# SAGE rounds of a graph network on transposed features, with the neighbour sum as one-hot products in PSUM

## The chip, the cores and the metric

The kernel runs on one core of a Trainium2 chip. The metric is the device time of one execution in microseconds; the median of three runs of the kernel before is 15,159.25 us (15,142.46 to 15,169.26). TensorE is PE here, VectorE DVE, ScalarE ACT, GpSimd POOL, SyncE SP.

## The reference, cut to what matters

There are 100,000 nodes with 128 features in f32 and 50,000 edges, sorted by destination. The destinations are drawn as 100,000 u^2, so that low nodes have many edges. Four blocks follow each other, each as `x = layernorm(x + block(x))`:

```python
# block 0: two SAGE layers, L2-normalised          (rounds 0 and 1)
agg = segment_sum(x[src], dst); cnt = segment_sum(ones, dst)
out = (agg / max(cnt, 1)) @ W_l + b_l + x @ W_r
h   = relu(out / max(norm(out), 1e-12))
# block 1: four SAGE layers without the norm        (rounds 2 to 5)
h = relu(agg * inv_deg @ W_l + h @ W_r + bias)
# block 2: attention with a softmax over each node's edges (round 6), block 3: transformer conv (round 7)
# then batch norm and the last layer norm           (output pass)
```

Rounds 0 to 5 are the six SAGE rounds; the layer norms of blocks 0 and 1 belong to rounds 1 and 5.

## The kernel before, in words

**Preparation.** The edges are loaded as a table of 98 blocks of 512. DVE, PE and POOL sort them by source in two passes (for round 6), and build index tables for gathers (`idx`), marks of equal neighbours (`keep`) and `inv`, one over the rank of an edge in its destination. `unit_end` says up to which unit of nodes the edges of a pair of blocks reach.

**A SAGE round** works in rows of nodes in DRAM and goes over 49 pairs of edge blocks (`schedule`, L377). For each pair POOL gathers source rows by indirect DMA, 128 rows an instruction (`gathers`, L592), PE transposes them into `edge_bank` (L731), DVE runs a scan along the edges (L1310: the running sum starts anew at each destination), PE multiplies by W_l (L737), ACT scales the rows by `inv` (L905), and POOL scatters those that close a destination into `agg` in DRAM (L603). SP waits until the scatters of the pair before have landed (L514) and only then loads.

**The dense part** goes in units of 1,024 nodes (98 of them, each two groups of 512 nodes, `s` = 0, 1) as soon as the edges below them are done. SP loads h (L520) and agg (L526) by groups, PE transposes h (L821), ACT copies it to SBUF (L968), PE adds bias (L827) and h W_r (L830), DVE adds the aggregate (L1428), and a tail follows by kind of round: norm, norm and layer norm, ReLU (ACT, L990), or ReLU and layer norm. ACT issues the stores (L961).

**Order.** Each engine runs its program in order. In an engine's program the pair comes first and then the units that it frees, so that a late unit holds up the next pair and the other way round. The tiles `h_in`, `agg_in`, `h_t`, `total`, `h_out` are doubled by `s` and are reused unit by unit. Rounds 6 and 7 (GAT and TR) have the same frame with a softmax in place of the scan. They keep their code in the change.

## Time and profile before

| | us |
|---|---|
| median of 3 runs | 15,159.25 |
| lowest, highest | 15,142.46, 15,169.26 |
| span of the profiled execution | 18,775.6 |
| PE busy in it | 9,112.1 (49%) |
| PE weight loads | 6,508.0 (35%) |
| DVE busy | 7,851.5 (42%) |
| POOL busy | 7,388.1 (39%) |
| ACT busy | 5,083.3 (27%) |
| DMA packets | 1,168,749, 2,071 MB, 110 GB/s |

The profiled execution has no other time than its span on record; what lies around the span isn't shown. The span is 3,616 us above the median of the other runs. Busy is the time in which the engine works on instructions; an engine that is idle may wait for another (then the profile names the releaser where it can) or for a DMA. "remote" and "issue" are waits for which it shows no releaser. The granted TensorE clock is a share of 2.4 GHz: 0.5 is 1.2 GHz; its mean over the run is 0.651.

### The profile page before, as it was taken

The numbers are of one execution on the slowest core, as the hardware profiler recorded it, in microseconds if no ns is written. First come the engines' busy times: TensorE is split into PE (matmuls) and PEld (weight loads), VectorE is DVE, ScalarE is ACT, GpSimd is POOL, SyncE is SP. The second block draws the span as 40 slices with busy tenths as digits, with TensorE's granted clock in tenths as the row PEclk, the third lists the DMA queues.
The fourth block names the chain that finished last, engine by engine and source line by source line (L and its number), as shares of the span: only waits on it lengthen the run. The fifth ranks groups of instructions, "written<-read, shape, count | busy, mean of one in ns | idle before, by whom it ended". The sixth has DMA issues, their size and how long they took to land. (4 is left out here: it accounts for less than half of the span.)

```text
span 18775.6 us, 221914 instructions
## 1 busy us (share of the span) xinstructions
PE 9112.1 (49%) x39191; PEld 6508.0 (35%) x39290; DVE 7851.5 (42%) x24729; ACT 5083.3 (27%) x12365; POOL 7388.1 (39%) x7460
## 2 busy tenths in 40 slices
...
GB/s 227 1 3 1 67 121 147 116 102 120 130 130 75 121 151 122 103 144 164 73 138 162 93 137 157 176 110 98 98 97 97 97 53 51 68 79 88 102 163 233
DMA packets 1168749, 2071.11 MB, mean 110 GB/s; under 512 B 283745, under 2 KB 292466, under 8 KB 1155794
## 3 DMA queue, kind: packets, MB, share of 16 engines
...
q14 instruction: 39, 0.32, 0.0%
...
HBM read 1358.91 MB, written 772.63 MB: 114 GB/s over the span
## 5 line engine op out<-in xcount | busy, mean ns | idle before, releaser
L603 POOL DMA_INDIRECT agg<-y_rows,s_idx x3136 | 3130.6, 998 | 1994.0 <-issue 1222.1
L827 PE MATMUL o_bank<-b_parts,ones_parts 3*128 3x512 bf16 (+1 forms) x1568 | 826.8, 527 | 4417.7 <-ACT h_t L968 2347.8
L830 PE MATMUL o_bank<-w_r,h_t 128*128 128x128 f32 x12544 | 2803.8, 393 | 0.0
L830 PEld LDWEIGHTS o_bank<-w_r,h_t 128*128 128x128 f32 x12544 | 2394.3, 285 | 577.3 <-issue 576.7
L1428 DVE TENSOR_TENSOR total<-o_bank,agg_in 128x512 f32<-128x512 f32 (+1 forms) x1568 | 1038.2, 688 | 3305.4 <-DMA agg_in<-agg 2001.8
L594 POOL DMA_INDIRECT gath<-node_a,g_idx x1176 | 1133.2, 964 | 2528.2 <-DVE g_idx L1292 1221.5
L968 ACT ACTIVATE h_t<-ht_bank 128x512 f32<-128x512 f32 (+1 forms) x1568 | 884.3, 593 | 3821.8 <-remote 2628.7
L827 PEld LDWEIGHTS o_bank<-b_parts,ones_parts 3*128 3x128 bf16 (+1 forms) x1568 | 150.5, 96 | 4800.6 <-ACT h_t L968 3073.7
L594 POOL DMA_INDIRECT gath<-node_b,g_idx x784 | 776.4, 990 | 2153.0 <-DVE g_idx L1292 1358.7
L594 POOL DMA_INDIRECT gath<-node_x,g_idx x784 | 782.7, 998 | 2052.7 <-DVE g_idx L1292 1161.4
L905 ACT ACTIVATE y_rows<-edge_bank,inv 128x128 f32<-128x128 f32 x2352 | 667.0, 369 | 2775.5 <-remote 1090.3
L1310 DVE TENSOR_TENSOR_SCAN run<-keep,run,edge_bank 128x512 f32<-128x512 f32 (+1 forms) x588 | 752.5, 1280 | 1307.6 <-PE edge_bank L731 604.1
L737 PE MATMUL edge_bank<-w_l,run 128*128 128x128 f32 x4704 | 895.2, 358 | 744.3 <-DVE run L1310 739.7
L821 PE MATMUL ht_bank<-ident,h_in 128*128 128x128 f32 x6272 | 1138.8, 339 | 230.1 <-issue 114.0
L582 POOL DMA_INDIRECT rec_dram<-rec_rows,place_idx x784 | 754.8, 963 | 1154.9 <-DVE rec_rows L1249 927.7
L1037 ACT ACTIVATE h_out<-t,small 128x128 f32<-128x128 f32 x2744 | 1096.9, 480 | 87.9 <-DVE small L1417 52.9
L821 PEld LDWEIGHTS ht_bank<-ident,h_in 128*128 128x128 f32 x6272 | 982.7, 182 | 366.0 <-issue 261.1
L737 PEld LDWEIGHTS edge_bank<-w_l,run 128*128 128x128 f32 x4704 | 800.7, 260 | 853.0 <-DVE run L1310 843.6
L731 PE MATMUL edge_bank<-ident,gath 128*128 128x128 f32 x2352 | 476.9, 361 | 813.8 <-DMA gath<-node_a,g_idx 403.0
L747 PE MATMUL edge_bank<-ident,run 128*128 128x128 f32 x784 | 218.6, 434 | 1318.7 <-DVE run L1347 1303.2
L1433 DVE TENSOR_REDUCE small<-zeros 128x4 f32<-128x512 f32 x392 | 262.1, 684 | 1157.1 <-ACT zeros L980 591.8
L731 PEld LDWEIGHTS edge_bank<-ident,gath 128*128 128x128 f32 x2352 | 398.2, 194 | 855.5 <-DMA gath<-node_a,g_idx 422.8
...
## 6 DMA issues: line engine op xcount, KB each, us to landing
...
node_x<-h_out ACTq DMA_DIRECT2D x390, 256.0 KB
h_in<-node_x SPq DMA_DIRECT2D x390, 256.0 KB
node_b<-h_out ACTq DMA_DIRECT2D x390, 256.0 KB
h_in<-node_b SPq DMA_DIRECT2D x390, 256.0 KB
...
```

The source lines that it names most:

```text
L582: pool.indirect_dma_start(rec_dram[n], bass.IndirectOffsetOnAxis(place_idx[q][:, k:k + 1], 0), rec_rows[q][:, k, :], None).then_inc(rec_ou ...
L594: pool.indirect_dma_start(gath[q][:, k, :], None, h_of, bass.IndirectOffsetOnAxis(g_idx[q][:, k:k + 1], 0)).then_inc(gathered[q], 16)
L603: pool.indirect_dma_start(agg[order(r)], bass.IndirectOffsetOnAxis(s_idx[q][:, k:k + 1], 0), y_rows[q][:, k, :], None, bounds_check=N - 1, ...
L731: last = pe.transpose(pe_bank[q][:, k * P:(k + 1) * P], gath[q][:, k, :], ident[:])
L737: last = pe.matmul(pe_bank[2 + q][:, k * P:(k + 1) * P], run[q][:, k * P:(k + 1) * P], w_l[r][:], start=True, stop=True, skip_group_check= ...
L821: last = pe.transpose(ht_bank[s][:, j * P:j * P + p], h_in[s][0:p, j, :], ident[0:p, 0:p])
L827: pe.matmul(o_bank[s][0:p, :], ones_parts[:, 0:p], b_parts[:, r, :].unsqueeze(1).to_broadcast([3, RPP, P]), start=True, stop=False, skip_g ...
L830: last = pe.matmul(o_bank[s][0:p, j * P:(j + 1) * P], h_t[s][:, j, 0:p], w_r[r][:], start=False, stop=j == RPP - 1, skip_group_check=True)
L968: act.activation(h_t[s][:, :, 0:p], ht_bank[s][:].rearrange("p (j n) -> p j n", j=RPP)[:, :, 0:p], ACT.Copy).then_inc(ht_ready[s], 1)
L1037: last = act.activation(h_out[s][0:p, j, :], of[s][0:p, j, :], ACT.Identity, scale=small2[s][0:p, 2 + 2 * turn, j:j + 1], bias=small2[s][0 ...
L1310: dve.tensor_tensor_scan(run[q][:], keep_of(i, q), pe_bank[q][:], run[1 - q][:, BLOCK - 1:BLOCK], ALU.mult, ALU.add).then_inc(run_ready[q], 1)
L1428: dve.tensor_tensor(flat(total[s], p), o_bank[s][0:p, :], flat(agg_in[s], p), ALU.add).then_inc(sum_ready[s], 1)
```

## The change

Rounds 0 to 5 get a program of their own; rounds 6 and 7 and the output pass stay, apart from names of semaphores.

- **Transposed features.** h is kept as columns in DRAM: for each of 196 groups a [128 features x 512 nodes] tile (`h_even`, `h_odd`, `n_cols`, `x_cols`), with node 4 p + j of the group at column 128 j + p. Loads and stores of it need no transpose. Round 0 has x in rows: PE transposes it and SP also stores it as columns, for the residual of round 1.
- **W_l at the writing side.** Beside the columns each round writes rows `y = h W_l(next round)`, 256 KB a group (`y_even`, `y_odd`), which the next round gathers. So the sum over neighbours needs no product any more. Round 0 gathers x itself and applies W_l after the sum. Round 5 writes plain rows (`node_b`) for round 6.
- **One-hot sums.** The edges are seen as 391 blocks of 128. For each group PE multiplies every block that touches it (`held`: gathered rows times 1 / degree, 128 x 128) by a one-hot matrix (`pick`: 128 edges x 512 nodes), both built by DVE, and adds into one PSUM bank; W_r h goes into the same bank (in round 0 into another). A block that spans a group's border is visited by both, 586 visits a round. How many blocks a group has is read from `visit_tab` by every engine at run time; the staged pairs lie in A, B, C0, C1, D0, D1, and DVE can be two visits ahead of PE.
- **POOL** only gathers: 392 indirect DMAs a round, eight at a time, into a ring of 32 blocks. There are no scatters and no `agg` in these rounds.
- **Statistics by PE.** Squared norms and variances are products with a column of ones, four a group; the reciprocals are spread over the features by products with a broadcast; the mean is taken off by a product with `centre`. ACT takes the square roots and squares, DVE the reciprocals and the products of whole tiles.
- **SP** issues all transfers of these rounds, stores too. The steps of a group are staggered over engines by fixed lags (`S_LAG` to `H_LAG`).
- `inv` becomes one over the degree for every edge of a destination (`end_f`), and the tables `dst_tab` and `visit_tab` are added.

```diff
+    EB = EPAD // P
+    LASTB = (E - 1) // P
+    VISITS = LASTB + GROUPS
+    RING = 32
...
+        def visits(eng, i, m, visit):
+            g = group_of(i, m)
+            place = visit_tab[0:1, g:g + 1] if isinstance(g, int) else visit_tab[0:1, bass.ds(g, 1)]
+            packed = eng.value_load(place, min_val=0, max_val=LASTB * 512 + 511)
+            lo, count = packed >> 9, packed & 511
...
+            visit(g, block_of(lo), f"C{m % 2}", True)
+            pairs = count >> 1
+            with eng.If(pairs > 0):
+                with eng.Fori(0, pairs) as n:
+                    visit(g, block_of(lo + (2 * n + 1)), "A", False)
+                    visit(g, block_of(lo + (2 * n + 2)), "B", False)
+            with eng.If((count & 1) > 0):
+                visit(g, block_of(lo + count), f"D{m % 2}", False)
...
+        S_LAG = {R_X: 2, R_NLN: 1}
+        C_LAG = {R_NLN: 2, R_RLN: 1}
+        T_LAG = {R_NLN: 3, R_RLN: 2}
+        O_LAG = {R_X: 1}
+        Y_LAG = {r: {R_X: 3, R_NLN: 4, R_RLN: 3}.get(r, 1) for r in sage_rounds}
+        H_LAG = {r: {R_X: 3, R_NLN: 4, R_RLN: 3}.get(r, 1) for r in sage_rounds}
...
+                            sp.wait_ge(o_mm[0], o_mm.at(r, g - 3))
+                            sp.sem_inc(sp_turn, 1)
+                            sp.dma_start(hin[q], cols_of(h_source[r], g)).then_inc(group_in[q], 16)
...
+                        cols_ready = relu_done if r in relu_sage else h_done
+                        sp.wait_ge(cols_ready[0], cols_ready.at(r, group_of(i, m) + 1))
+                        sp.sem_inc(sp_turn, 1)
+                        sp.dma_start(cols_of(h_target[r], group_of(i, m)), h_cols[m % 2]).then_inc(h_cols_out[m % 2], 16)
...
+                        sp.wait_ge(y_done[0], y_done.at(r, group_of(i, m) + 1))
+                        sp.sem_inc(sp_turn, 1)
+                        sp.dma_start(rows_of(y_table[r + 1], group_of(i, m)), as_cols(y_out[m % 2])).then_inc(y_rows_out[m % 2], 16)
...
+            def eight_blocks(r, d, turn_of_ring):
+                done = r * EIGHTS + d
+                pool.wait_ge(released, (done + 1) * 8)
+                pool.sem_inc(pool_turn, 1)
+                near = near_idx[turn_of_ring]
+                pool.tensor_copy(near[:].rearrange("p (b k) -> p b k", k=CPB),
+                                 idx[0][:, bass.ds(2 * d, 2), 0:CPB]).then_inc(copied, 1)
+                pool.wait_ge(copied, done + 1)
+                pool.sem_inc(pool_turn, 1)
+                for half in range(2):
+                    for k in range(half * 4, half * 4 + 4):
+                        pool.indirect_dma_start(ring[:, turn_of_ring * 8 + k, :], None, y_table[r],
+                                                bass.IndirectOffsetOnAxis(near[:, k:k + 1], 0)).then_inc(blocks_in[half], 16)
+                    if half == 1:
+                        pool.wait_ge(blocks_in[0], (done + 1) * 64)
+                        pool.sem_inc(block_ready, 4)
...
+                def visit_into(bank):
+                    def visit(g, b, name, first):
+                        pe.wait_ge(staged, r * VISITS + b + g + 1)
+                        pe.matmul(bank[:], held[name], pick[name], start=first, stop=False, skip_group_check=True).then_inc(used, 1)
...
+                        pe.matmul(bank[:], w_r[r][:], hin[m % 4], start=False, stop=True, skip_group_check=True).then_inc(o_mm[0], 1)
...
+                def column_sums(bank, of, weight):
+                    for j in range(RPP):
+                        last = pe.matmul(bank[:, j:j + 1], of[:, j * P:(j + 1) * P], weight[:], start=True, stop=True,
+                                         skip_group_check=True)
...
+                def spread(bank, values):
+                    for j in range(RPP):
+                        last = pe.matmul(bank[:, j * P:(j + 1) * P], values[:, j:j + 1].to_broadcast([P, P]), ident[:],
+                                         start=True, stop=True, skip_group_check=True)
...
+                def step(i, k):
+                    if r in two_norm and running(i, k - S_LAG[r]):
+                        square_sums(i, k - S_LAG[r])
+                    if r in two_ln and running(i, k - C_LAG[r]):
+                        centred(i, k - C_LAG[r])
+                    if running(i, k):
+                        aggregated(i, k)
+                    if r == R_X and running(i, k + 1):
+                        x_columns(i, k + 1)
+                    if r in two_norm and running(i, k - S_LAG[r]):
+                        unit_spread(i, k - S_LAG[r])
+                    if r == R_X and running(i, k - 1):
+                        both_products(i, k - 1)
+                    if r in two_ln and running(i, k - C_LAG[r]):
+                        variances(i, k - C_LAG[r])
+                    if r in two_ln and running(i, k - T_LAG[r]):
+                        scale_spread(i, k - T_LAG[r])
+                    if running(i, k - Y_LAG[r]):
+                        next_rows(i, k - Y_LAG[r])
...
+                def visit(g, b, name, first):
+                    dve.wait_ge(block_ready, r * EB + b + 1)
+                    dve.wait_ge(used, r * VISITS + b + g + 1)
+                    slot = (b + r * EB) & (RING - 1)
+                    scaled = dve.tensor_scalar(held[name], ring[:, bass.ds(slot, 1), :].rearrange("p o f -> p (o f)"),
+                                               column(inv_tab, b), None, ALU.mult)
+                    if not first:
+                        scaled.then_inc(released, 1)
+                    dve.tensor_scalar(pick[name], iota_node[:], column(dst_tab, b), column(group_off, g),
+                                      ALU.subtract, ALU.is_equal).then_inc(staged, 1)
...
+                def step(i, k):
+                    if running(i, k):
+                        visits(dve, i, k, visit)
+                    if r in two_norm and running(i, k - S_LAG[r]):
+                        unit_scales(i, k - S_LAG[r])
+                    if r in two_ln and running(i, k - T_LAG[r]):
+                        scales(i, k - T_LAG[r])
+                    if r in two_norm and running(i, k - S_LAG[r]):
+                        unit_rows(i, k - S_LAG[r])
+                    s_lag = S_LAG[r] if r == R_NLN else 0
+                    if r in two_ln and running(i, k - s_lag):
+                        residual_sum(i, k - s_lag)
+                    if r in two_ln and running(i, k - T_LAG[r]):
+                        normalised(i, k - T_LAG[r])
...
-                    for step, q in ((gathers, 0), (gathers, 1), (scatters, 0), (scatters, 1)) if kind != SAGE else (
-                            (gathers, 0), (scatters, 0), (gathers, 1), (scatters, 1)):
...
-                def sage_pair(i, r=r):
```

On ACT a group costs: round 0 a square root, the copy of the sum, the copy of the transposed x, square, ReLU, copy of the next rows; round 1 square root, square and copy of the centred tile, square, ReLU, square root, next rows; a ReLU round ReLU and next rows.

## Rows read from the trace of the kernel before

**Rows 1.** Stages: window, us, busy by engine (instructions), clock, DMA share, GB/s
```profile
270.00:1958.30 1688.30, 968.39 (x3900) 365.18 (x3998) 932.02 (x3571) 0.00 (x0) 754.79 (x784) 0.72 0.03 6
1958.30:3578.70 1620.40, 789.73 (x3724) 634.25 (x3724) 628.82 (x1864) 369.73 (x982) 769.26 (x784) 0.65 0.39 121
3578.70:5763.70 2185.00, 900.66 (x3724) 731.64 (x3724) 1014.21 (x4021) 802.90 (x2149) 769.68 (x784) 0.60 0.37 114
5763.70:10438.30 4674.60, 2293.36 (x11172) 1837.11 (x11172) 852.58 (x1477) 992.00 (x2359) 2306.79 (x2352) 0.67 0.41 127
10438.30:12249.30 1811.00, 846.03 (x3724) 679.47 (x3724) 744.88 (x2846) 566.60 (x1569) 772.68 (x784) 0.63 0.44 141
12249.30:15125.80 2876.50, 1140.81 (x4508) 844.69 (x4508) 2081.50 (x6666) 1295.79 (x3039) 788.39 (x784) 0.58 0.32 98
15125.80:18775.60 3649.80, 2170.78 (x8428) 1413.37 (x8428) 1569.51 (x4222) 1053.57 (x2257) 1224.02 (x1176) 0.67 0.34 104
1958.30:12249.30 10291.00, 4829.77 (x22344) 3882.47 (x22344) 3240.47 (x10205) 2731.24 (x7058) 4618.41 (x4704) 0.64 0.40 126
```
**Rows 2.** Waits in rounds 2 to 4: us in total, times, longest us
```profile
DVE total L1428 <- DMA agg_in<-agg: 1477.1, 274, 21.7
ACT h_t L968 <- remote: 1401.5, 222, 14.4
POOL gath L594 <- PE edge_bank L731: 1275.5, 100, 26.3
```
**Rows 3.** One transfer in POOL's timeline, round 3: start, us, operation, idle before
```profile
7954.85 1.02 POOL L603 DMA_INDIRECT agg<-y_rows,s_idx  x1 [0.30 <-issue]
```
**Rows 4.** Timeline of SP's transfers in round 2
```profile
6497.68 0.92 SPq L526 DMA_DIRECT2D agg_in<-agg  x2
6506.85 4.93 SPq L520 DMA_DIRECT2D h_in<-node_x  x2
6516.80 4.94 SPq L526 DMA_DIRECT2D agg_in<-agg  x2
```
**Rows 5.** Timeline of PE in round 6
```profile
13505.65 1.71 PE L749 MATMUL edge_bank<-head_pick,den 128*128 128x4 f32 x8
...
13512.40 1.88 PE L767 MATMUL edge_bank<-gsrc_t,w_t 128*128 128x512 f32 x4
13514.11 1.04 PE L821 MATMUL ht_bank<-ident,h_in 128*128 128x128 f32 x8
...
13516.05 1.16 PE L830 MATMUL o_bank<-w_r,h_t 128*128 128x128 f32 x8
```
**Rows 6.** Single lines: duration ns min/median/max, first and last start, forms
```profile
L1443 DVE TENSOR_SCALAR h_out<-total,small x784: 267/282/548, 2141.4 to 3578.5; 128x128 f32<-128x128 f32 x195, 40x128 f32<-40x128 f32 x1
...
L1177 DVE TENSOR_SCALAR keep<-keep x1: 426/426/426, 273.4 to 273.4; 98x512 f32<-98x512 f32 x1
...
L1224 DVE TENSOR_SCALAR keep<-keep x784: 283/343/551, 461.3 to 1901.2; 128x512 bf16<-128x512 f16 x98, 128x264 bf16<-128x264 f16 x98
...
L1428 DVE TENSOR_TENSOR total<-o_bank,agg_in x1568: 673/691/694, 2131.1 to 18107.7; 128x512 f32<-128x512 f32 x196
...
L990 ACT ACTIVATE h_out<-total x784: 612/629/633, 5944.5 to 18108.4; 128x512 f32<-128x512 f32 x196
```
**Rows 7.** DVE's operations of the sorter's line L1218 in 20 us of the trace
```profile
300.00:320.00 20.00, 16.29 (x47) 1.00 0.00 0
```
**Rows 8.** Line L385 (the read of a table at run time), sequencer of DVE
```profile
L385 DVEq TENSOR_LOAD <-unit_end x384: 299/309/1033, 1974.3 to 17980.2; - x192
```
**Rows 9.** Stretches as in group 1: sorting twice, then the output pass
```profile
320.00:440.00 120.00, 116.37 (x488) 54.41 (x557) 98.15 (x279) 0.00 (x0) 0.00 (x0) 1.00 0.00 0
1173.00:1280.00 107.00, 96.86 (x722) 58.07 (x720) 84.45 (x386) 0.00 (x0) 10.64 (x12) 0.96 0.00 0
18530.00:18630.00 100.00, 54.50 (x240) 48.89 (x240) 70.23 (x360) 74.73 (x180) 0.00 (x0) 0.53 0.74 235
```
**Rows 10.** Line L594, the gathers: duration ns min/median/max
```profile
L594 POOL DMA_INDIRECT gath<-node_a,g_idx x1176: 942/953/1128, 3581.4 to 12108.4; - x196
```

675 lines of the change are left out of this document (506 added, 169 removed).

## The prediction

> **What bounds the kernel now.** I read the stages first, then who waits in them, then single operations. The stages [rows 1] cut the profiled span of 18,776 us at the start of each round: 270 us of loading and zeroing, 1,688 us of sorting, six SAGE rounds, 2,877 us for the attention round, 3,650 us for the transformer round with the output pass. The SAGE rounds take 10,291 us, and they are all that the change rebuilds; the reader is to see that in them no engine is busy for more than half of the time (PE 4,830, POOL 4,618, DVE 3,240, ACT 2,731 us). So they are bound by waits. In the three plain ReLU rounds [rows 2] DVE waits for the aggregate to come back from DRAM (1,477 us of 4,675), ACT for a transposed tile whose load is late (1,402 us, releaser not seen), POOL for the transposes behind the dense units on PE's in-order queue (1,276 us). That is a chain through DRAM: gather, scan, scatter, then load of what was scattered.
>
> A floor under it is POOL: 16 gathers and scatters for each of 49 pairs at 1.28 us each (0.98 busy on average, 4,618 us for 4,704 of them [rows 1], and 0.30 of issue [rows 3]) are 784 x 1.28 = 1,004 us in every round, against 1,558 us for a ReLU round.
>
> One thing must be said of the profile. Its span is 24% over the median of the timed runs (15,159 us); no row shows what lies around the span. Where the excess sits is partly seen [rows 4]: two loads that SP normally issues in 0.92 us take 4.93 and 4.94 us, while POOL is in the middle of its gathers. I come back to this, as it decides the sign.
>
> **The change, priced.** Removed from the rounds: the scans, the 392 scatters of a round, the reload of the aggregate, the transposes of each dense unit, and all unit statistics on DVE. Added: 390 + 196 = 586 visits a round (a block of 128 edges against a group of 512 nodes), and dense work for 196 groups in transposed form.
>
> PE, at its full clock. The nearest rows [rows 5]: four 512-column f32 instructions go by in 13514.11 - 13512.40 = 1.71 us, and an f32 product is two of them, so 0.86 us; four 128-column products (8 instructions) last 1.04 to 1.16 us with the tail of the last, 0.9 from start to start. Column sums (8 weight loads, hardly any columns) are 1.71 us at the low clock, so about 0.85 at the full one. By group, with 2.99 visits on average:
> - ReLU round: 3.99 x 0.86 (visits, W_r) + 0.9 (next rows) = 4.33 us; x196 = 849 us, three times.
> - Round 0: 4.99 x 0.86 (visits, W_r, W_l) + 3 x 0.9 (transposes, spread, next rows) + 0.85 (sums) = 7.84; 1,537 us.
> - Round 1: 4.99 x 0.86 (visits, W_r, centring) + 2 x 0.85 + 3 x 0.9 = 8.69; 1,703 us.
> - Round 5: 4.99 x 0.86 + 0.85 + 2 x 0.9 = 6.94; 1,360 us.
> Together 3 x 849 + 1,537 + 1,703 + 1,360 = 7,147 us. Nothing hides this: it is one engine in order. The bounds are the full clock (7,147) and the low clock throughout (twice that).
>
> DVE, visits. One multiplication of 128x128 f32 with a column as scalar is 282 ns; the comparison over 512 columns is 426 ns with constants, some 45 more with two columns as operands [rows 6], so 0.28 + 0.47 = 0.75 us. Register work comes on top: the sorter's loop issues 47 such operations in 20 us [rows 7], 0.43 us each where one lasts 0.35, so 0.08 for each. With two waits I take 1.05 us a visit, between 0.75 (all registers hidden) and 1.3. Per group the visit table is read: 0.31 us for the load, then unpacking, two branches and a loop [rows 8], 1.3 us taken, between 0.5 and 2.1. So 2.99 x 1.05 + 1.3 = 4.4 us in a ReLU round, as much as PE has. With only two buffers for a staged visit (`used` starts at 2) the two engines can't fully even out; I add 0.4 us a group there. In round 0 DVE has 0.17 + 0.17 + 0.69 more, in round 1 0.52 + 3 x 0.69, in round 5 0.17 + 2 x 0.69: under PE's sums, but DVE stands still for PE's spread products, and what is queued behind on DVE is the next group's first visit, for which PE then waits. I add 0.2, 0.5 and 0.5 us. Sum: 0.4 x 588 + 0.2 x 196 + 0.5 x 392 = 470 us.
>
> ACT has at most six 512-column passes of 0.6 us a group [rows 6], 3.6 us, and is hidden under PE everywhere; without PE's cover it would be the limit of no round. SP now issues the stores too: three transfers (four in round 0) at 0.6 us each with their registers, 1.9 to 2.5 us a group, hidden. If SP goes slow as in [rows 4], the three groups loaded ahead cover some 13 us; the stores have two buffers, so ACT's rectified tile and, behind it, PE's next product would wait. DMA: 0.79 MB a group in 4.4 us is 180 GB/s; the output pass moves 235 GB/s at a share of 0.74 [rows 9], so hidden.
>
> POOL: 392 gathers x 1.28 = 502 us and 49 copies with waits, about 575 us a round, under every round. But destinations are crowded at low nodes (their density falls as one over the root of the position), so the first 15 groups need some 107 blocks, and there POOL's 1.4 us a block exceeds the visit's 1.05: 40 us a round. Each round also drains its stores and fills the ring, 35 us. Together 6 x 75 = 450 us.
>
> After: 7,147 + 470 + 450 = 8,067 us for the SAGE rounds against 10,291. The table work before them is one-off and small (some 20 operations under 1 us, inside 1,688 us). In the profile's own time that is 18,776 - 10,291 + 8,067 = 16,552 us.
>
> **A rule that speaks against it.** The longest case of the one-column multiplication is 548 ns against 282 typical, and of the sorter's comparison 551 against 343 [rows 6], and the sorter's fell beside POOL's transfers: DVE and POOL do disturb each other here, by up to 0.27 us. The visits put two such operations beside POOL's gathers all the time. The Trainium skill (SBUF — State Buffer, "SBUF: two separate sides") says that a VectorE operation in a two-port mode takes a port pair exclusively, so that GpSimd can't write descriptors until it ends; its own example is a transfer of 620 ns that takes 3,100. By that factor a gather would take five times as long. By the rows, the 1,176 gathers from node_a last 0.94 to 1.13 us [rows 10], so POOL's side hardly shows it; I charge nothing for it in the sum and keep it as rival 4.
>
> **From the profile to the timed runs.** The rest of the program shrinks by 15,159 / 18,776 = 0.807 if the excess is spread evenly: 8,485 becomes 6,850 us. PE's instruction rate cannot shrink, the other 920 us of the new rounds can: 7,147 + 743 = 7,890. Sum 14,740 us, 2.8% faster. That is the forecast.
>
> **Rivals.**
> 1. *The excess sits in the old SAGE rounds* (slower). Then they take far less than 8,309 us when timed, and the new PE-bound rounds replace something cheap. The point is 7,890: if more than 2,401 of the 3,617 us of excess is theirs, the change loses. For it: the slow SP issues [rows 4] are in these rounds beside POOL's bursts, and late loads are what the rounds wait for [rows 2]. Against: POOL alone needs 1,004 us in each, 6,024 in all, rounds 1 and 5 have long DVE chains above it, and 1,688 us of sorting also run beside POOL. With 3,000 us of it there: 15,159 + (7,890 - 7,291) = 15,760 us.
> 2. *PE doesn't hold its full clock* (slower). The granted clock is 1.00 in a stretch in which PE is busy for 97%, 0.96 at 91%, 0.53 at 54% [rows 9]; the SAGE rounds now have 0.64. If the two-buffer handshake leaves PE at 80% busy and the clock at 0.8 on average, PE's 7,147 become 8,930: 16,500 us. It decides from a mean clock under 0.94 (7,147 / (7,147 + 419)). The forecast has PE busy for 89%, so the rows speak for a clock near 1. The Trainium skill (TensorE: Matmul & The Clock Gate, "HAM oscillation — how this bites in real kernels") tells of loops whose regular waits throw the array back to half rate; the trace agrees where waits are long.
> 3. *The visits are cheaper, and the old profile stretches all alike* (faster): everything goes by 0.807, (8,485 + 8,067) x 0.807 = 13,360 us. For it: register and semaphore work is what a profile would stretch; against: matmul spacing is not.
> 4. *POOL starves the visits*: each gather waits for a whole comparison of DVE, 1.28 + 0.47 = 1.75 us. 686 us a round is still hidden later on, but the crowded groups get 107 x 0.47 us more, 300 us in all: 15,040 us. For it: the stretched operations of [rows 6]; against: [rows 10]. By the factor of five in the Trainium skill's example (SBUF — State Buffer) POOL would bind every round at 392 x 6.4 us, and the time would be near 22,000 us; no row is near that.
>
> **How the numbers follow.** Forecast 0.50, rival 1 0.21, rival 2 0.10, rival 3 0.12, rival 4 0.07. A measurement of this kernel tells 0.2%, some 30 us, from no change. The forecast's own range is 14,100 to 15,400: DVE's visit at 0.75 or 1.3 us takes 235 us off or puts 280 on in the ReLU rounds, and the waits on spread products and round ends (about 680 us of the sum) can be none or twice that, not all on one side together. A tenth of it lies above 15,190. Faster: 0.42 of the forecast, rivals 3 and 4, together 0.61. Same: 0.03 of the forecast and 0.02 of rivals 1 and 2. Slower: 0.05 and 0.29, together 0.34. The range takes in most of rivals 1 and 3: 13,400 to 16,100.
>
> **What would show it.** Right: ReLU rounds near 1,000 us and rounds 0, 1, 5 near 1,650, 1,880, 1,540; PE busy over 85% in them with a clock over 0.95; a visit's cadence of 1.0 to 1.1 us. Wrong: PE waiting for the comparison with DVE over 90% busy (my visit is too cheap); a clock near 0.7 (rival 2); DVE waiting for `ring` past the first 15 groups, or gathers well over 1.3 us (rival 4); ACT waiting for h_cols or y_out stores (SP). If the profiled rounds come out at 8,000 to 8,500 us and the timed run is still slower, rival 1 is right.

## The result: 3.1% slower where it was first compared, 2.3% faster on another chip

| | kernel before, us | kernel after, us | after / before |
|---|---|---|---|
| first comparison (4 runs each) | 15,150.85 (15,129.81 to 15,169.26) | 15,622.35 (15,607.41 to 15,638.28) | 1.0309 [1.0297, 1.0321] |
| a later one, on another chip | 18,445.97 (7 runs) | 18,022.38 (4 runs) | 0.977 [0.9749, 0.9791] |

The forecast of 14,740 us was wrong, and in sign: the change costs 3.1% where it was to be measured. The kernel before takes 15,150 to 15,170 us on some chips and 18,450 to 18,790 us on others, within 0.4% in each set of runs, and each ratio below compares two kernels on one chip. I call them the quick and the slow chips; whether it is the chip itself or what runs beside it there, the runs don't tell. The profile that the prediction rests on has the span of a slow one (18,776 us), the times beside it are those of a quick one. The unaltered changed kernel ran on one chip of each kind.

The stages of the changed kernel on a quick chip (window, us, busy time of PE, PEld, DVE, ACT, POOL with instructions, PE's clock, DMA share, GB/s), cut at the starts of the rounds: the sorting, rounds 0, 1, 2, 5, then all six SAGE rounds.

```profile
270.00:1635.00 1365.00, 907.02 (x4008) 349.34 (x4008) 939.94 (x3594) 0.94 (x2) 752.84 (x785) 0.82 0.03 3
1635.70:3345.50 1709.80, 1643.29 (x7836) 1021.45 (x7836) 637.40 (x1760) 610.45 (x1176) 391.62 (x442) 1.00 0.41 135
3345.50:5216.30 1870.80, 1818.30 (x9796) 1204.82 (x9796) 921.51 (x2348) 663.19 (x1372) 390.59 (x441) 1.00 0.40 124
5216.30:6169.20 952.90, 902.00 (x3132) 454.50 (x3132) 448.21 (x1172) 251.73 (x392) 393.71 (x441) 0.99 0.59 189
...
8071.70:9764.80 1693.10, 1515.75 (x6660) 849.69 (x6660) 734.23 (x1760) 516.01 (x980) 392.69 (x440) 1.00 0.35 106
...
1635.70:9764.80 8129.10, 7684.98 (x33688) 4441.23 (x33688) 3634.96 (x9384) 2544.82 (x4704) 2355.51 (x2645) 1.00 0.46 145
```

Against [rows 1] the picture is another one: TensorE is busy for 95% of the six rounds at a granted clock of 1.00 (before: 47% at 0.64, and 57% at 0.73 in the quick profile below), and POOL's 784 transfers a round have become 441 operations (392 gathers, 49 copies). The rounds take 8,129 us, 0.8% from the 8,067 of the sum. Yet the kernel is slower, since on this chip the old rounds were not the 10,291 us of [rows 1]. Below is a second profile of the kernel before, from a quick chip (span 15,168.7 us; the same columns; rounds 0, 1, 2 and 5, then all six):

```profile
1634.90:2811.30 1176.40, 723.95 (x3724) 584.33 (x3724) 627.39 (x1865) 367.56 (x982) 768.52 (x784) 0.75 0.52 167
2811.30:4597.80 1786.50, 836.96 (x3724) 682.91 (x3724) 1016.43 (x4021) 801.63 (x2149) 767.95 (x784) 0.65 0.45 139
4597.80:5749.70 1151.90, 708.63 (x3724) 570.57 (x3724) 289.04 (x494) 337.89 (x791) 767.40 (x784) 0.74 0.53 171
...
8019.60:9332.40 1312.80, 751.87 (x3724) 605.38 (x3724) 748.34 (x2846) 571.92 (x1570) 781.97 (x784) 0.72 0.59 195
...
1634.90:9332.40 7697.50, 4400.31 (x22344) 3552.99 (x22344) 3260.49 (x10205) 2748.63 (x7058) 4620.62 (x4704) 0.73 0.52 168
```

Round by round, from these two tables (after less before, quick chips): round 0 +533 us (1,710 against 1,176), round 1 +84, rounds 2 to 4 -199, -185 and -182, round 5 +380. The six together +432, and the rest of the program 7,504 against 7,471. That is the 464 us between the spans (15,632.7 and 15,168.7). What was won in the ReLU rounds (566 us) is less than what rounds 0 and 5 lose (913 us).

Where PE's time goes in a round that loses can be read in its groups in round 0 of the changed kernel (line, engine, operation, tile, count | busy us, mean ns | idle before them and what ended it):

```profile
L979 PE MATMUL edge_bank<-keep 128*128 128x512 f32 x1172 | 598.2, 626 | 57.1 <-DVE keep L1750 39.5 <-issue 12.8
L990 PE MATMUL ht_bank<-ident,node_small 128*128 128x128 f32 x1568 | 207.4, 275 | 1.4 <-DVE node_small L1759 1.4
L1067 PE MATMUL edge_bank<-w_l,keep 128*128 128x128 f32 x1568 | 206.7, 275 | 0.8 <-ACT keep L1314 0.8
L984 PE MATMUL edge_bank<-one_col,keep 128*128 128x1 f32 x1568 | 206.1, 253 | 1.6 <-ACT keep L1286 1.6
L1036 PE MATMUL o_bank<-t,w_l 128*128 128x512 f32 x392 | 200.2, 592 | 0.0
```

The visits are only 598 of the 1,710 us. A norm in transposed form costs PE 413 us of busy time a round that it did not have before: 206 for the sums of squares (L984, one output column from each weight load of 128) and 207 to spread one value a node over its 128 features (L990). Before, DVE and ACT did this, and PE was busy for 62% of round 0. That this work is why round 0 loses is a sum of busy times, not a test; the last set of experiments speaks against it for the sums of squares.

### The profile page after: what moved, and what is told of

It reads as the page before. It is cut to its first block, busy times and chain, and to the rows that moved or that the text cites. A ratio compares the mean times of both kernels' runs of the same rounds, so it can differ in the third digit from the quotient of the medians.

```text
span 15632.7 us, 266007 instructions
## 1 busy us (share of the span) xinstructions
PE 11691.0 (75%) x50643; PEld 6945.8 (44%) x50644; DVE 8242.4 (53%) x23933; ACT 4902.6 (31%) x10013; POOL 5131.3 (33%) x5404
## 4 chain that ended last, share of the span: by engine, by line
PE 49%; DVE 19%; issue 11%; DMA 5%; DVEq 5%; POOL 5%; ACT 4%; SPq 1%; ACTq 1%; another core or an unknown queue 0%; POOLq 0%
PE o_bank L979 13%; PE o_bank L1019 5%; PE edge_bank L1067 5%; PE ht_bank L990 5%; PE edge_bank L984 3%; DVE keep L1750 3%; POOL rec_dram L782 3%; PE edge_bank L979 3%; DVE st L1934 2%; ACT t L1444 2%; PE edge_bank L934 2%; DVE seg_max L1855 2%; DVE full_max L1858 2%; DVE run L1882 2%; ACT h_out L1466 2%
## 5 line engine op out<-in xcount | busy, mean ns | idle before, releaser
L979 PE MATMUL o_bank<-keep 128*128 128x512 f32 x5860 | 3054.1, 624 | 372.2 <-DVE keep L1750 329.0
L1746 DVE TENSOR_SCALAR keep<-keep,inv 128x128 f32 x3516 | 1056.2, 300 | 2597.1 <-PE o_bank L979 1236.9
L1750 DVE TENSOR_SCALAR keep<-iota_node,dst_tab,group_off 128x512 f32<-128x512 f32 x3516 | 1947.8, 554 | 0.5 <-issue 0.4
L979 PEld LDWEIGHTS o_bank<-keep 128*128 128x128 f32 x5860 | 924.9, 190 | 2053.1 <-DVE keep L1750 1851.9
L799 POOL DMA_INDIRECT keep<-y_even,near_idx x1176 | 1142.2, 971 | 449.6 <-issue 316.8
L1067 PEld LDWEIGHTS edge_bank<-w_l,keep 128*128 128x128 f32 x7840 | 1013.8, 192 | 374.5 <-issue 364.7
L1067 PE MATMUL edge_bank<-w_l,keep 128*128 128x128 f32 x7840 | 1033.8, 275 | 1.6 <-ACT keep L1314 1.6
L843 POOL DMA_INDIRECT agg<-y_rows,s_idx x784 | 777.0, 991 | 707.0 <-DVE s_idx L1843 476.9
L799 POOL DMA_INDIRECT keep<-y_odd,near_idx x784 | 763.8, 974 | 303.4 <-issue 209.4
L990 PE MATMUL ht_bank<-ident,node_small 128*128 128x128 f32 x6272 | 860.0, 280 | 1.4 <-DVE node_small L1759 1.4
L990 PEld LDWEIGHTS ht_bank<-ident,node_small 128*128 128x128 f32 x6272 | 777.8, 190 | 95.7 <-issue 93.3
```

What stands on the lines that cost most here:

```text
L799: pool.indirect_dma_start(ring[:, turn_of_ring * 8 + k, :], None, y_table[r], bass.IndirectOffsetOnAxis(near[:, k:k + 1], 0)).then_inc(blo ...
L843: pool.indirect_dma_start(agg[order(r)], bass.IndirectOffsetOnAxis(s_idx[q][:, k:k + 1], 0), y_rows[q][:, k, :], None, bounds_check=N - 1, ...
L979: pe.matmul(bank[:], held[name], pick[name], start=first, stop=False, skip_group_check=True).then_inc(used, 1)
L990: last = pe.matmul(bank[:, j * P:(j + 1) * P], values[:, j:j + 1].to_broadcast([P, P]), ident[:], start=True, stop=True, skip_group_check= ...
L1067: last = pe.matmul(bank[:, j * P:(j + 1) * P], h_cols[m % 2][:, j * P:(j + 1) * P], weight[:], start=True, stop=True, skip_group_check=True)
L1746: scaled = dve.tensor_scalar(held[name], ring[:, bass.ds(slot, 1), :].rearrange("p o f -> p (o f)"), column(inv_tab, b), None, ALU.mult)
```

## The experiments

**First set, on a quick chip: where did the old kernel's time lie?** Rival 1 of the prediction says that the excess of the first profile sits in the old SAGE rounds. All four are the kernel before, or parts of it.

Unaltered, profiled again. 

> The kernel before, unchanged, profiled a second time. Its first profile has a span of 18,776 us where its timed runs take 15,151 us; the profile of the changed kernel has 15,633 us where it takes 15,622 us. Theory A (the excess of 3,617 us is an accident of one profiled execution): the span is now near 15,160 us, SP's pairs of transfers take 0.92 us everywhere, and the ReLU rounds are far under 1,558 us. Theory B (it belongs to this kernel under a profiler): the span is again near 18,800 us, with the same slow transfers beside POOL's bursts. Timed: 15,151 us in either case.

Measured: 15,166.93 us, ratio 1.0006 [0.9995, 1.0016]; its span is 15,168.7 us. So a profile does not stretch the kernel, and what theory A foretold holds. (The first profile is no accident of one execution, though: the later sets time this kernel at 18,446 to 18,794 us on other chips.) The register work that SP does before a load (L388) shows where the two profiles differ, first in the first profile, then here (count: shortest, median, longest ns):

```profile
L388 SPq FUSED_REGOPS  x724: 3/41/1395, 2124.9 to 18020.0; - x181
L388 SPq COMPARE_BRANCH  x724: 4/45/1425, 2139.5 to 18027.7; - x181
```
```profile
L388 SPq FUSED_REGOPS  x724: 41/41/51, 1775.3 to 14415.3; - x181
L388 SPq COMPARE_BRANCH  x724: 34/45/50, 1778.0 to 14421.2; - x181
```

The medians agree, the tails don't. Of the register and branch instructions in the old SAGE rounds, 901 of SP's 9,972 and 491 of ACT's 10,379 took over 0.45 us in the first profile (some 0.7 each), and none in the second.

The SAGE rounds left out.
```diff
-        (SAGE, "norm", x_in, None, node_a, ...),        # and the other five SAGE rows of ROUNDS
-        (GAT, "gat", node_b, node_b, node_x, ...),
+        (GAT, "gat", x_in, x_in, node_x, ...),
```


> The kernel before without its six SAGE rounds: round 6 reads x, all else stays. Theory 1 (the excess of the profile lay in the old SAGE rounds, these were cheap when timed): what is left takes what the same stages take in the profile of the changed kernel, 270 + 1,365 + 2,811 + 3,057 = 7,503 us, and the old SAGE rounds took 15,151 - 7,503 = 7,648 us. Theory 2 (the excess was spread evenly, and the changed kernel made the stages after it slower): 0.807 x 8,485 = 6,850 us, and the old SAGE rounds took 8,300 us.

Measured: 7,466.72 us (7,461.32 to 7,468.13), ratio 0.4928 [0.4919, 0.4936]. The old SAGE rounds are worth 15,157 - 7,467 = 7,690 us, not 8,309, if nothing overlaps at their ends.

Rounds 3 and 4 left out, and rounds 0 and 1 left out.
```diff
-        (SAGE, "relu", node_a, None, node_b, ...),
-        (SAGE, "relu", node_b, None, node_a, ...),
...
-        (SAGE, "norm", x_in, None, node_a, ...),
-        (SAGE, "norm_ln", node_a, x_in, node_x, ...),
-        (SAGE, "relu", node_x, None, node_a, ...),
+        (SAGE, "relu", x_in, None, node_a, ...),
```


> The kernel before with two of its three ReLU rounds left out (rounds 3 and 4; round 5 reads what round 2 wrote). Theory 1: a ReLU round is near POOL's floor of 784 x 1.28 = 1,004 us, say 1,030, so 15,151 - 2,060 = 13,090 us. Theory 2: a ReLU round takes 0.807 x 1,558 = 1,257 us, so 12,640 us. In the changed kernel it takes 952 us.

> The kernel before without rounds 0 and 1 (round 2 and the residual of round 5 read x). Together they take 3,581 us in the changed kernel. Theory 1: the old SAGE rounds sum to 7,648 us, of which 3 x 1,030 for ReLU rounds and some 1,500 for round 5, which leaves 3,060 us for these two: 12,090 us, so that nearly all of the loss is here (round 0 at 1,060 against 1,710 us). Theory 2: 0.807 x 3,805 = 3,071 us, 12,080 us. The two theories agree here; the run sizes rounds 0 and 1, and with the two other cuts also round 5.

Measured: 12,901.55 us (ratio 0.8522 [0.8507, 0.8536]) and 12,199.53 us (0.8055 [0.8041, 0.8068]): 1,128 us for a ReLU round, 2,957 for rounds 0 and 1, as in the second profile (1,135 and 2,963). A ReLU round had shrunk from 1,558 us to 1,135, by 0.728, not by the 0.807 that I gave to everything.

**Second set: what bounds the new rounds?** These are the changed kernel with one thing altered. They ran on a slow chip, where the kernel before took 18,460.34 us (7 runs); the changed kernel's own time to set beside them, 18,022, comes from the third set, on another slow chip whose kernel before stood at 18,446, so a difference of some tens of us says nothing.

The comparison of a visit over 128 of 512 nodes.
```diff
-   dve.tensor_scalar(pick[name], iota_node[:], ...
+   dve.tensor_scalar(pick[name][:, 0:P], iota_node[:, 0:P], ...
```


> From the changed kernel. VectorE's comparison of a visit is made over 128 of the 512 nodes of the group (the other 384 columns of the one-hot block stay zero, so most of the edge sums are left out); all other instructions, TensorE's full-width products among them, stay. In the profile of the changed kernel the comparison takes 554 ns on average, 3,516 times (1,948 us). Theory P (TensorE's own sum sets the SAGE rounds: it is busy 95% of them): VectorE waits longer, the time stays within 100 us of 15,620, as the ReLU rounds stay at about 950 us; at most the 175 us that TensorE idles in round 5 shrink. Theory V (the visits' hand-shake through VectorE sets them): about 0.4 us off each of 3,516 visits, 14,200 to 14,500.

Measured: 17,905.62 us, ratio 0.9689 [0.9673, 0.9706], 117 us under the changed kernel. DVE's comparison fell from 549 to 348 ns, 709 us of its work in all, and the time by a sixth of that. Theory V is out as it stood, and theory P's limit of 100 us is just passed.

A visit's product over 256 of 512 columns.
```diff
-   pe.matmul(bank[:], held[name], pick[name], ...
+   pe.matmul(bank[:, 0:GROUP // 2], held[name], pick[name][:, 0:GROUP // 2], ...
```


> From the changed kernel. TensorE's product of a visit covers 256 of the 512 columns of its PSUM bank (half of the edge sums is left out); VectorE's work stays whole. The product's two instructions take 614 to 646 ns each in the profile, 7,032 of them. Theory P: each pair loses up to 256 columns twice at full clock; by the 128x512 products (592 ns an instruction) against the 128x128 ones (275 ns for four times fewer columns) some 0.4 us a visit, 3,516 visits: 1,100 to 1,500 us off, 14,100 to 14,500, a ReLU round near 750. Theory V: no more than 150 us off, since VectorE's part of a visit is whole.

Measured: 17,561.37 us, ratio 0.9502 [0.9486, 0.9518], 461 us less: more than V's 150, far from P's 1,100.

bf16 for the squares and the columns that sum them.
```diff
-   one_col, mean_col = sb("one_col", [P, 1]), sb("mean_col", [P, 1])
+   one_col, mean_col = sb("one_col", [P, 1], BF16), sb("mean_col", [P, 1], BF16)
-   squares = [in_ring([GROUP]) for k in range(2)]       # and squares2
+   squares = [in_ring([GROUP], BF16) for k in range(2)]
```


> From the changed kernel. The squares whose sums over the features TensorE takes (one sum in the norm, one in the layer norm) are written in bf16, and their ones and 1/128 columns are bf16: each sum is then four bf16 products with four weight loads, where the f32 one is eight of each. In the profile a sum of a group takes 1.05 us of TensorE (1,568 instructions, 206.1 us in 196 groups), mostly for weight loads, and there are four such sums in rounds 0, 1 and 5 (784 groups together, 823 us). Theory P, with the norms' small products as what the norm rounds lose: a sum falls to 0.3 to 0.5 us, so 400 to 600 us off: 15,000 to 15,200, round 1 alone by 200 to 300, the ReLU rounds unchanged. Theory W (the extra time of rounds 0 and 5 is waiting between engines, not TensorE's work): under 100 us off.

Measured: 17,682.99 us, ratio 0.9565 [0.9547, 0.9584], 339 us less. In round 0 the sums went from 209.6 us on PE to 49.3, as these two lines show (the changed kernel, then this one):

```profile
L984 PE MATMUL edge_bank<-one_col,keep 128*128 128x1 f32 x1568 | 209.6, 255 | 33.6 <-ACT keep L1286 32.8 <-issue 0.8
```
```profile
L985 PE MATMUL edge_bank<-one_col,keep 128*128 128x1 bf16 x784 | 49.3, 167 | 31.7 <-ACT keep L1287 30.1 <-issue 1.6
```

That is 0.8 us of PE's busy time a sum and some 640 us in all, of which the time gave back about half: beside the changed kernel of the third set 156 us in round 1 and 155 in round 5, but 17 in round 0 (1,911 for 1,928).

A visit as two bf16 products, the block split in high and low part.
```diff
-   scaled = dve.tensor_scalar(held[name], block, inv, None, ALU.mult)
+   dve.tensor_scalar(held[name][:, 0, :], block, inv, None, ALU.mult).then_inc(hot, 1)
+   dve.wait_ge(hot, ...)
+   scaled = dve.scalar_tensor_tensor(held[name][:, 1, :], block, inv, held[name][:, 0, :], ALU.mult, ALU.subtract)
-   dve.tensor_scalar(pick[name], iota_node[:], ...     # f32
+   dve.tensor_scalar(pick[name], iota_half[:], ...     # fp16 in, bf16 out
-   pe.matmul(bank[:], held[name], pick[name], ...
+   pe.matmul(bank[:], held[name][:, 0, :], pick[name], ...
+   pe.matmul(bank[:], held[name][:, 1, :], pick[name], ...
```


> From the changed kernel. The scaled block of a visit is split on VectorE into two bf16 blocks (high part, and the rest), the one-hot block is written as bf16 from an fp16 row of node numbers, and the visit is two bf16 products in place of an f32 one, in all six SAGE rounds. Theory P: two bf16 products of 512 columns take TensorE about half of the f32 one's 1.25 us; 0.4 to 0.6 us off 3,516 visits; where the gathers (784 a round at 0.97 us, 760 us) or VectorE (three instructions a visit and a wait for its own result) don't catch it, 1,200 to 1,600 us off, ReLU rounds 760 to 850 us; forecast 14,300. Theory V: VectorE has one instruction and one wait more in each visit, the time rises by 500 to 1,000 us, unless its bf16 comparison is faster than 554 ns.

Measured: 18,257.59 us, ratio 0.9875 [0.9857, 0.9894], 235 us more than the changed kernel, though PE's busy time fell by 1,085 us (12,531 to 11,445). That is far from theory P and short of theory V. The third instruction costs DVE 351 ns, the bf16 comparison still takes 410.

**Third set, on another slow chip: does the sign hang on the chip?** The changed kernel again, the bf16 sums with a later layer norm in round 5, the high and low products again, all three together.
```diff
-   C_LAG = {R_NLN: 2, R_RLN: 1}
-   T_LAG = {R_NLN: 3, R_RLN: 2}
+   C_LAG = {R_NLN: 2, R_RLN: 2}
+   T_LAG = {R_NLN: 3, R_RLN: 3}      # Y_LAG and H_LAG of R_RLN 4, s_lag 1
```


> The changed kernel, unaltered, beside the kernel before. The last four kernels ran where the kernel before took 18,460 us, against 15,160 in the runs before them, and in their profiles some 1,060 to 1,130 of 40,700 register, branch and wait instructions of VectorE's sequencer and some 840 to 870 of SyncE's took over 0.45 us (median 0.04 us), against none and 16 in the profile of the changed kernel at 15,633 us. Theory M (a property of the chip or of what runs beside it, which stretches both kernels by a different amount, so that the sign of the change hangs on it): where the kernel before takes about 18,460 us, this one takes 18,100 to 18,400, the ratio 0.98 to 1.00, since its rounds 2 to 4 were 1,190 us there in the comparison over 128 nodes and rounds 0 and 5 some 1,900; where the kernel before takes about 15,160 us, the ratio is 1.030 again. Theory N (the changed kernel is 3% slower everywhere): 19,000 us at a kernel before of 18,460.

> The changed kernel with the squares and their columns in bf16 (as in the run of the bf16 sums) and round 5's layer norm one group later at each step, as in round 1. Theory P (TensorE's sum bounds the rounds, and round 5 loses 180 us more to a chain inside one group): where the kernel before takes 15,160 us, the sums give 400 to 600 us and the lag 50 to 150: 14,900 to 15,150, that is level with the kernel before or just below it; rounds 0, 1 and 5 at about 1,560, 1,570 and 1,400 us. Where the kernel before takes 18,460, it stays within 150 us of the run with the sums alone, 17,680. Theory W (waits between engines): the sums give under 100 us and only the lag counts.

> The changed kernel with the visits as two bf16 products (high and low part of the block), as run before. Where the kernel before took 18,460 us its rounds 2 to 4 took 1,240 us each, TensorE 65% busy and VectorE 46%, with 315 us a round in which VectorE's next block waited for nothing but its own sequencer. Theory D (a visit costs VectorE some 1.4 us in all: 0.29, 0.35 and 0.41 us of work and the registers and waits between, and this takes TensorE's place as the bound): where the kernel before takes 15,160 us, rounds 2 to 4 come to 586 visits x 1.4 = 820 to 950 us, the whole to 15,000 to 15,500. Theory P (TensorE's sum alone): 1,200 to 1,600 us off, 14,000 to 14,400.

> The changed kernel with all three: bf16 sums, bf16 high and low visits, round 5's layer norm one group later. Where the kernel before takes 15,160 us: by theory D, VectorE's 1.4 us a visit sets a floor of about 820 us in every round, and the norm rounds, where TensorE has 1,100 to 1,250 us of work left, gain both: 14,200 to 14,700. By theory P 13,600 to 14,000. Where the kernel before takes 18,460: the two bf16 products are no gain there, 17,500 to 17,900.

Measured, with the kernel before at 18,445.97 us: 18,022.38 (0.977 [0.9749, 0.9791]), 17,695.31 (0.958 [0.9554, 0.9607]), 18,230.55 (0.9875 [0.9855, 0.9895]) and 17,959.24 us (0.9733 [0.9713, 0.9753]). Theory M holds and its ratio was still a little too high: here the change gains 2.3%. The lag gives nothing here (17,695 against 17,683; round 5 takes 1,790 us with it and 1,795 with the sums alone), the three together are worse than the sums alone (17,500 to 17,900 was expected). The stages of the changed kernel here, rounds 0, 1, 2 and 5 and all that follows them (columns as above):

```profile
1928.00:3856.00 1928.00, 1722.63 (x7832) 1061.62 (x7832) 635.46 (x1760) 610.23 (x1175) 389.97 (x442) 0.94 0.36 120
3856.00:5988.00 2132.00, 1912.72 (x9796) 1243.59 (x9796) 922.09 (x2348) 656.70 (x1372) 389.64 (x442) 0.94 0.35 108
5988.00:7169.00 1181.00, 980.05 (x3132) 482.48 (x3132) 447.69 (x1172) 249.65 (x392) 391.41 (x442) 0.92 0.47 152
...
9565.00:11515.00 1950.00, 1627.23 (x6660) 922.16 (x6660) 734.50 (x1760) 513.65 (x980) 387.11 (x436) 0.92 0.30 92
11515.00:18018.60 6503.60, 3335.53 (x12936) 2255.36 (x12936) 3647.94 (x10888) 2353.59 (x5296) 2017.83 (x1960) 0.63 0.33 103
```

The new SAGE rounds go from 8,129 to 9,587 us (18% more), the old ones from 7,697 to 10,291 (34%). DVE's queue shows what does it, at the line that scales a block (quick chip, then this one):

```profile
L1746 DVEq ALU_OP  x6446: 40/45/50, 1644.0 to 9747.9; - x196
L1746 DVE TENSOR_SCALAR keep<-keep,inv x3516: 285/286/535, 1644.2 to 9748.1; 128x128 f32 x196
```
```profile
L1746 DVEq ALU_OP  x6446: 1/45/1408, 1929.1 to 11496.7; - x196
L1746 DVE TENSOR_SCALAR keep<-keep,inv x3516: 268/286/536, 1929.4 to 11496.9; 128x128 f32 x196
```

DVE's work on data takes what it took in the median; its register arithmetic has a tail. In the SAGE rounds 789 of DVE's 33,631 register and branch instructions took over 0.45 us (553 us together) and 421 of SP's, where the quick chip has none. The two engines hand visits to each other over two staging places, so PE's next product waits too. The granted clock goes with it: 0.92 over these rounds for 1.00, and PE's busy time grows from 7,685 to 8,218 us for the same instructions, 533 of the 1,458 us that are added.

**Fourth set, on a third slow chip** (kernel before 18,475.79 us).

> The changed kernel with the bf16 sums and round 5's layer norm one group later, as before, where the kernel before took 18,446 us and this one 17,695, against 18,022 for the changed kernel. Where the kernel before takes 15,160 us: theory P (TensorE's sum bounds the SAGE rounds there, 95% busy in them): 784 sums of about 0.6 us less are 470 us, more than the 327 us measured above, and the lag 50 to 150 us: 14,950 to 15,150. Theory W (waits between engines): 15,400 to 15,600. Where it takes 18,450: 17,700 again.

> The changed kernel with two bf16 products a visit, as before, where it cost 208 us more than the changed kernel (18,231 against 18,022). Where the kernel before takes 15,160 us: theory D (VectorE's part of a visit takes over as the bound, 1.06 us of work in three instructions and 0.3 to 0.4 us of registers, branches and the wait for its own result): ReLU rounds 820 to 950 us, in all 15,000 to 15,600. Theory P (TensorE alone): 14,000 to 14,400. Where it takes 18,450: 18,230 again.

> The changed kernel with the product of a visit over 256 of its 512 columns (half of the edge sums left out), as before, where it took 17,561 us, 461 less than the changed kernel. Where the kernel before takes 15,160 us: theory P: TensorE's busy time falls by some 250 us in each of six rounds, and the time by 1,100 to 1,500 us less what VectorE's visits (0.85 us of work and 0.3 to 0.4 us of registers and branches, 586 a round, 700 us) and the gathers (784 x 0.97 = 760 us a round) hold up: ReLU rounds at 760 to 800 us, in all 14,400 to 14,800. Theory V: within 150 us of 15,620. Where it takes 18,450: 17,560 again.

Measured: 17,707.04 (0.9577 [0.9552, 0.9602]), 18,282.18 (0.9891 [0.9863, 0.9919]) and 17,593.27 us (0.952 [0.9499, 0.9542]). They repeat the earlier ones within 0.3% and tell nothing of a quick chip.

**Fifth set: take the gathers away.** In the SAGE rounds of the third set's changed kernel, 85% of DVE's 789 slow instructions start within 1 us, before or after, of the start of one of POOL's indirect transfers, where 28% of all its register instructions do. So the gathers go, and with them, if that is the cause, the difference between the chips. All visits after the first 32 blocks read those blocks again, and the waits for the landings are set to be met at once.
```diff
+   first_ring = r == 0 and isinstance(d, int) and d < 4
...
-   for k in range(half * 4, half * 4 + 4):
+   for k in range(half * 4, half * 4 + 4 if first_ring else half * 4):
        pool.indirect_dma_start(ring[:, turn_of_ring * 8 + k, :], None, y_table[r], ...
...
-   pool.wait_ge(blocks_in[0], (done + 1) * 64)
+   pool.wait_ge(blocks_in[0], (done + 1) * 64 if first_ring else 256)      # and so for blocks_in[1]
```


> The changed kernel with 3,104 of its 3,136 gathers of the SAGE rounds left out: only the ring's first 32 are made, and all later visits read those blocks again, so the edge sums are wrong in every round; everything else stays. Where the kernel before takes 18,450 us and the changed kernel 18,022, its SAGE rounds take 9,590 us, with 710 slow register instructions of VectorE in them. Theory G (the slow register instructions are caused there by POOL's indirect DMAs running beside them): they vanish from the SAGE rounds, TensorE is busy 95% of them again, and they take 8,100 to 8,300 us: 16,500 to 16,700 in all. Rival H (the chip's sequencers are slow for another reason): they stay, 17,700 to 18,100. Where the kernel before takes 15,160: under theory P (TensorE's sum) the time stays within 150 us of 15,620; if the gathers held the rounds up, more goes.

> The same without those gathers, with the visits as two bf16 products. Against the run without gathers alone, whichever the chip, if theory G holds: theory D (VectorE's visit, 1.06 us of work and 0.3 to 0.4 us of registers, branches and waits, becomes the bound): ReLU rounds at 820 to 900 us in place of 950, 300 to 700 us off in all. Theory P (TensorE alone): its busy time falls by some 250 us a round, 1,200 to 1,500 off. Theory V (VectorE bounds the visits already): 500 us more.

> The same without those gathers, with the bf16 sums and round 5's layer norm one group later. Against the run without gathers alone: theory P: rounds 0, 1 and 5 lose 0.6 us for each of 784 sums and round 5 another 50 to 150 us: 450 to 620 us off, ReLU rounds unchanged. Theory W (waits between engines): under 150 us.

Measured, with the kernel before at 18,794.37 us: 16,514.26 (0.8785 [0.8771, 0.88]), 16,744.9 (0.8911 [0.8896, 0.8926]) and 16,222.54 us (0.864 [0.8624, 0.8656]). First the run with nothing but the gathers gone: rounds 0, 1, 2 and 5.

```profile
1951.70:3652.00 1700.30, 1649.43 (x7832) 1023.03 (x7832) 631.32 (x1760) 609.88 (x1175) 39.09 (x76) 0.99 0.35 121
3652.00:5508.00 1856.00, 1815.75 (x9796) 1204.46 (x9796) 915.86 (x2348) 663.10 (x1372) 11.79 (x49) 1.00 0.35 111
5508.00:6442.00 934.00, 900.07 (x3132) 455.14 (x3132) 438.23 (x1172) 251.72 (x392) 11.63 (x49) 1.00 0.49 165
8309.00:9980.00 1671.00, 1511.82 (x6622) 845.17 (x6623) 728.22 (x1757) 513.97 (x977) 11.80 (x49) 1.00 0.29 92
```

On a slow chip these are the quick chip's times with gathers, less 0.6 to 2% (1,700 for 1,710, 1,856 for 1,871, 934 for 953, 1,671 for 1,693), at a clock of 0.99 to 1.00, and 19 slow instructions of DVE's are left in them for 789. Theory G is shown: the slow register instructions of the SAGE rounds come with POOL's indirect transfers, on chips where they come at all. Whether with their issuing or with the traffic that they make, this run doesn't part. It speaks as well for the gathers being no bound of the changed kernel on a quick chip; no run without them was made there. The sorting, whose scatters stay, keeps its slow instructions (359 of 4,834).

The other two, rounds 2 and 5 with the high and low products and round 0 with the bf16 sums:

```profile
5482.00:6447.00 965.00, 714.50 (x3079) 350.64 (x3132) 563.96 (x1758) 252.06 (x392) 9.52 (x49) 0.96 0.47 160
...
8383.00:10225.00 1842.00, 1403.16 (x6539) 859.23 (x6637) 856.90 (x2345) 514.86 (x978) 9.49 (x49) 0.88 0.27 83
```
```profile
1951.00:3652.00 1701.00, 1499.03 (x7048) 865.44 (x7048) 631.08 (x1760) 588.22 (x1175) 37.67 (x75) 0.99 0.35 121
```

With the high and low products PE loses 186 us of work in round 2 and the round takes 31 us more. Most of their cost is in round 5, which takes 171 us more at a clock of 0.88; round 0 takes 77 less. With the bf16 sums PE loses 150 us in round 0 and the round stays as it was; round 1 gave back 141 of 228 us, round 5, with the lag, 134 of 138. So PE at 95% busy was not alone. In round 0 of that last run (engine, tile, line it waited for: us, times, longest us) DVE waits in every group for the spread product, and PE for DVE's comparison:

```profile
DVE keep L1770 <- PE ht_bank L992: 594.2, 196, 3.5
...
PEld edge_bank L981 <- DVE keep L1752: 332.9, 357, 8.0
```

Visits, spread product, DVE's product of the tile, next visits: that ring does not hold the sums of squares, which would explain why making them cheaper gave nothing there. It is read from the order of the two programs and these waits; no run took it apart.

Beside PE stands DVE's part of a visit, which shows in two stretches of DVE's timeline, the f32 visits and the high and low ones (start, us, operation, idle before and what ended it):

```profile
6002.01 0.28 DVE L1747 TENSOR_SCALAR keep<-keep,inv 128x128 f32 x1 [0.75 <-issue]
6002.21 0.54 DVE L1751 TENSOR_SCALAR keep<-iota_node,dst_tab,group_off 128x512 f32<-128x512 f32 x1
6003.13 0.29 DVE L1747 TENSOR_SCALAR keep<-keep,inv 128x128 f32 x1 [0.38 <-issue]
```
```profile
6001.90 0.29 DVE L1750 TENSOR_SCALAR keep<-keep,inv 128x128 bf16 x1 [0.63 <-issue]
6002.22 0.35 DVE L1752 SCALAR_TENSOR_TENSOR keep<-keep,inv 128x128 bf16<-128x128 bf16 x1
6002.49 0.41 DVE L1756 TENSOR_SCALAR keep<-iota_half,dst_tab,group_off 128x512 bf16<-128x512 f16 x1
6003.95 0.29 DVE L1750 TENSOR_SCALAR keep<-keep,inv 128x128 bf16 x1 [1.05 <-PE o_bank L982]
```

A visit is here 1.12 us of DVE from start to start without a wait for PE (6002.01 to 6003.13), 0.38 of it idle with no releaser seen, where its register instructions run, and the first visit of a group has 0.63 to 0.75 of it. With two visits staged at most, DVE stops while PE does a group's dense products (1.8 us from the first of W_r, by PE's own timeline there), and PE then waits for DVE. So both wait in turn. In round 2 of the high and low run (engine, tile, line it waited for: us, times, longest us):

```profile
PEld o_bank L981 <- DVE keep L1756: 455.2, 425, 5.2
...
PE o_bank L981 <- DVE keep L1756: 234.4, 372, 1.2
DVE keep L1750 <- PE o_bank L982: 224.4, 201, 2.2
```

Of my theories for these two runs none was right in size: high and low cost 231 us (D said 300 to 700 less, P 1,200 to 1,500 less, V 500 more), the sums with the lag gave 292 (P said 450 to 620, W under 150). How much a third and fourth staging buffer would give back wasn't tried.

Which version is best: on slow chips the one with bf16 sums and the later layer norm, 4.2% under the kernel before (0.958 and 0.9577), with the sums alone as good. On a quick chip none of the altered versions ran. An estimate from the runs without gathers, whose rounds are near those of a quick chip, is 15,622 - 292 = 15,330 us, still above the kernel before's 15,151. So no version is shown to beat the kernel before on both kinds of chip.

## Why the prediction was wrong

1. *From the profile to the timed runs* is the step that failed. It shrank everything but PE's work by one factor, 0.807, as if the excess of the profile were spread evenly. The rest of the program was to go from 8,485 to 6,850 us; measured are 7,467 (the rounds left out) and 7,504 (the profile after). The new rounds were to go from 8,067 to 7,890; measured are 8,129. Against the span of 15,633 us the forecast of 14,740 lacks 893: 654 in the rest, 239 in the rounds, and 177 of these are the shrinking again, only 62 the sum itself. By the same factor the old rounds came to 8,309; they take 7,690. The excess sat unevenly: 2,594 us of 3,607 in the old SAGE rounds (10,291 less 7,697), beyond the turning point of 2,401 that rival 1 names.
2. *Rival 1* (chance 0.21) is right in where the excess sits and in the sign. That its price of 15,760 us is only 0.9% high is luck: it took 3,000 us of excess and 7,890 us for the new rounds. With the 2,594 measured its own sum gives 15,352, and the 239 us missing in the rounds bring it near. Its reason, late loads beside POOL's bursts [rows 4], fits the slow instructions of SP in the first profile and their absence in the second; no run took the transfers away from the old rounds.
3. *The new rounds* by kind, predicted and measured: ReLU 1,000 and 952, round 0 1,650 and 1,710, round 1 1,880 and 1,871, round 5 1,540 and 1,693. Together they are within 0.8% of the sum of 8,067.
4. *PE's terms* came to 7,147 us and PE is busy for 7,685. The terms for products that follow each other at once were right: by the starts below, 0.86 us for W_r and 0.89 for the next rows (0.86 and 0.9 taken). A visit behind a wait takes 0.97.

```profile
5704.44 1.12 PE L979 MATMUL o_bank<-keep 128*128 128x512 f32 x2 [0.27 <-DVE keep L1750]
5705.41 1.02 PE L1019 MATMUL o_bank<-agg_in,w_r 128*128 128x512 f32 x2
5706.27 1.05 PE L1067 MATMUL edge_bank<-w_l,keep 128*128 128x128 f32 x8
5707.16 1.05 PE L979 MATMUL o_bank<-keep 128*128 128x512 f32 x2
```

   Counted so over whole rounds, idle time left out, a visit is 0.96 us in round 2, 0.99, 1.03 and 1.08 in rounds 0, 1 and 5, for 0.86 taken. That is some 480 of the 538 us. The rest: in round 0 the transposes of x took 0.49 us a group for 0.9, the sums 1.03 for 0.85, and a closing product (`no_row`, L1015) of 0.31 us was not in the sum at all; in rounds 1 and 5 the sums took 0.81. The clock held 1.00, rival 2 is out.
5. *DVE's visits and the allowances.* The comparison with two columns as operands is 549 to 554 ns for 0.47 us taken, and the visit's 1.05 us is 1.12 in the stretch shown above. For hand-shake and round ends I had put 470 + 450 = 920 us; PE idles for 444 (8,129 less 7,685). So 538 too little and 476 too much nearly cancel. I call it luck in part only: the visits' excess is largest in round 5, where PE's weight loads wait for the comparison in all 586 visits (651 us), so it may be the hand-shake seen as busy time. That is argued; no run takes the two apart. Round 5 has 1,516 us of work for the 1,360 taken and idles another 177, 158 of it for DVE's comparison. I had blamed the layer norm, chained inside its group there; the run with the lag undoes the chain and round 5 gained 5 us on slow chips, so the cause of that idle time stays open.
6. *SP's slow issues* [rows 4] were read as a risk of stores and priced at nothing for DVE. On a slow chip the same thing falls on 789 of DVE's 33,631 register and branch instructions, and the new rounds take 9,587 us there, not 8,067. The profile's own sum (16,552 us) would have been 18,019.
7. *POOL* is hidden, as said: without its gathers the rounds take 8,028 us for 8,129, though on another chip. Gathers last 0.971 us on average beside the visits' operations on DVE (`L799`, the first line below), and the longest of the 1,305 that DVE was working beside for over 60% of their time lasts 1.43; rival 4 is out, and so is, here, the factor of five in the example of the Trainium skill (SBUF — State Buffer, "SBUF: two separate sides"). On slow chips it isn't the gather that gets longer either (second line), but DVE's register work beside it. In the DMA sum the 0.79 MB a group leaves out the gathers: 189 GB/s over the 4.86 us of a group in round 2 are 0.92 MB.

```profile
L799 POOL DMA_INDIRECT keep<-y_even,near_idx x1176 | 1142.2, 971 | 449.6 <-issue 316.8 <-POOL near_idx L793 118.9 <-DMA keep<-y_even,near_idx 10.4
```
```profile
L799 POOL DMA_INDIRECT keep<-y_even,near_idx x1176 | 1138.6, 968 | 449.8 <-issue 341.5 <-POOL near_idx L793 104.3 <-DMA keep<-y_even,near_idx 4.0
```

Why the old rounds are stretched more than the new (34% against 18%) is argued, not tested: they have the slow instructions on SP and ACT (1,392 in all), at the head of a chain gather, scan, scatter, load in which every link is waited for [rows 2], and 784 indirect transfers a round beside them against 392.
